# One transformer layer on eight cores: the mean of |W| for three weights is taken during attention and output projection, and the ternarizing of a weight strip is spread between token blocks

## The reference

```
x = x + attn(layernorm(x), Wq, Wk, Wv, Wo)      # 16 heads of 128, rope, causal softmax
x = x + ffn(layernorm(x), w_gate, w_up, w_down)  # d_ffn = 8192

def _weight_quant(w):                  # three values: -scale, 0, +scale
    scale = clip(mean(|w|), 1e-5)
    return clip(round(w / scale), -1, 1) * scale
def _act_quant(x):                     # 8-bit integers per token
    scale = 127 / clip(max(|x|, last axis), 1e-5)
    return clip(round(x * scale), -128, 127) / scale
ffn: gate = bl(x, w_gate); up = bl(x, w_up); out = bl(silu(gate) * up, w_down)
     where bl(x, w) = einsum(act_quant(x), weight_quant(w))
```

## Time and profile before

| | us |
|---|---|
| median of the runs before (2 runs, 11487.83 to 11526.1) | 11506.97 |
| the profiled execution | 11501.9 |
| its span, on the slowest core (core 3; the 8 cores: 11405.9 to 11500.3) | 11500.3 |
| attention, from 2421 us of the span | 2671 |
| output projection, from 5092 us | 585 |
| the means, from 5677 us | 697 |
| gate and up: first strip ternarized, from 6374 us | 179 |
| gate and up, from the first matmul at 6553 us | 2797 |
| down, from 9350 us | 2150 |

### The profile page before, as it was taken

One profiled execution on the slowest core, in us unless ns is written; L12 is line 12 of the kernel. 1 busy time (PEld: TensorE's weight loads), 2 busy tenths in 40 slices (PEclk: granted clock), 3 DMA queues, 4 the chain that ended last, 5 costly groups with the idle time before them and its releaser, 6 DMA issues.

```text
span 11500.3 us, 91991 instructions; the slowest of 8 cores (11405.9 to 11500.3 us)
## 1 busy us (share of the span) xinstructions
PE 5967.9 (52%) x23698; PEld 2265.1 (20%) x23698; DVE 4138.7 (36%) x5258; ACT 1951.3 (17%) x3620; POOL 1254.3 (11%) x587
## 2 busy tenths in 40 slices
PE   0025664965665566555200165756657556363737
PEld 0012221421111111112100022322323222131313
DVE  3513332132222222216675344444444441405050
ACT  4541110013333333331000000000000010101010
POOL 0002121000000000000000323233232300000000
PEclk9999898977777777777655587878878777575857
DMA  2251423310000000023496524233233313332333
GB/s 103 93 129 37 75 54 64 75 44 22 22 13 22 22 22 13 22 46 102 145 338 241 157 97 120 91 114 109 95 121 97 101 62 122 97 123 95 132 95 115
DMA packets 618721, 1048.40 MB, mean 91 GB/s; under 512 B 337394, under 2 KB 419314, under 8 KB 568818
## 3 DMA queue, kind: packets, MB, share of 16 engines
q1 hardware_dynamic: 441444, 656.54, 19.2%
q10 hardware_dynamic: 168192, 352.40, 8.9%
q0 software_dynamic: 8592, 33.59, 1.8%
HBM read 807.51 MB, written 218.10 MB: 89 GB/s over the span
## 4 chain that ended last, share of the span: by engine, by line
PE 36%; DVE 25%; DMA 11%; ACT 9%; issue 8%; POOL 6%; SPq 2%; ACTq 2%; DVEq 1%; another core or an unknown queue 1%; POOLq 0%
PE pb L68 27%; ACT p_E L68 3%; PE p2S L68 3%; DVE p_hqt L68 3%; PE p4b L68 3%; SPq L68 2%; ACT p_dump L68 2%; DVE p_pm L68 2%; DVE p4a_tmp L68 2%; DVE p_invr L68 2%; DVE p_wf L68 2%; DMA p_wf<-wgT 2%; ACTq L68 2%; DMA p4a_w<-wdT 2%; DMA p_wf<-wuT 1%
## 5 line engine op out<-in xcount | busy, mean ns | idle before, releaser
L68 PE MATMUL pb<-p_wgt,p_xiT 128*128 128x512 bf16 x4096 | 961.2, 389 | 1167.8 <-DVE p_ht L68 987.4
L68 PE MATMUL pb<-p_wds,p_hTg 128*128 128x512 bf16 x4096 | 999.5, 413 | 263.5 <-DMA p_wds<-wdtd 263.5
L68 ACT ACTIVATE p_E<-pb,p_negB 128x512 bf16<-128x512 f32 x1280 | 879.7, 687 | 788.6 <-PE pb L68 628.8
L68 PE MATMUL p2S<-p_E,g_ones_colb 128*1 128x512 bf16 x1280 | 539.1, 421 | 483.4 <-DVE p_E L68 254.8
L68 DVE TENSOR_TENSOR p_E<-p_E,p_masks 128x512 bf16<-128x512 bf16 x512 | 218.1, 426 | 1470.3 <-ACT p_E L68 1470.1
L68 PEld LDWEIGHTS pb<-p_wgt,p_xiT 128*128 128x128 bf16 x4096 | 408.3, 100 | 1681.2 <-issue 1221.9
L68 DVE TENSOR_SCALAR p_pm<-p_wf,p4a_invtau 128x2048 f32<-128x2048 f32 x192 | 407.7, 2123 | 718.5 <-DMA p_wf<-wdT 261.8
L68 PE MATMUL pb<-k_pp_xT,k_pp_W 128*128 128x512 bf16 x2048 | 476.9, 388 | 289.0 <-ACT k_pp_qb L68 185.2
L68 ACT ACTIVATE p_sg<-pb,p_cg 128x512 f32<-128x512 f32 x256 | 175.9, 687 | 2524.0 <-DVE p_cu L68 1559.9
L68 PEld LDWEIGHTS pb<-p_wds,p_hTg 128*128 128x128 bf16 x4096 | 426.0, 104 | 835.9 <-issue 571.6
L68 PE MATMUL pb<-p_qT,p_kT 128*128 128x512 bf16 x1280 | 560.1, 448 | 0.0
(11 more groups left out here) (158 smaller groups left out, 6652.3 us busy)
## 6 DMA issues: line engine op xcount, KB each, us to landing
p_wds<-wdtd ACTq DMA_DIRECT2D x128, 1024.0 KB, 5.2
p4a_w<-wgT SPq DMA_DIRECT2D x16, 4096.0 KB, 15.7
p4a_w<-wuT SPq DMA_DIRECT2D x16, 4096.0 KB, 15.2
p4a_w<-wdT SPq DMA_DIRECT2D x64, 1024.0 KB, 5.9
p_wf<-wdT SPq DMA_DIRECT2D x64, 1024.0 KB, 6.6
p_wf<-wgT SPq DMA_DIRECT2D x64, 1024.0 KB, 6.0
p_wf<-wuT SPq DMA_DIRECT2D x64, 1024.0 KB, 5.3
hfpd<-p_ht ACTq DMA_DIRECT2D x256, 256.0 KB, 2.0
```

What stands on the lines that cost most here:

```text
L68: real = getattr(eng, meth)(*a, **k)
```

## The change

Two things are changed.

The first: stage 4 is gone. Its sums are taken in 192 chunks of 128 x 2048, each by a load on SP (`wa_t`, two buffers), one ACT instruction with the function Abs that also gives the sum over the columns (`wa_tmp`), and one small ACT instruction that adds it (`wa_acc`). Five chunks are recorded at the end of each head in stage 2 and seven at the end of each token block in stage 3, 80 and 112 in all. The few instructions that turn the sums into thresholds come at the end of stage 3.

The second: in stage 5 the 12 items of strip fw+1 are no longer recorded ahead of the token blocks of strip fw, but one behind each of its first 12 blocks.

```diff
+    wa_state = {"i": 0, "rel": [(sS, 0), (sS, 0)], "first": True}
+    def wa_chunk(mi, wd, r0, c0, W):
...
+        slw = i % 2
+        sem = [dm["wa0"], dm["wa1"]][slw]
+        wait(Y, wa_state["rel"][slw])
+        sem.inc(Y.dma_start(wa_tile[slw][:, :W], wd.ap()[r0:r0 + 128, c0:c0 + W]), 16)
+        toks = [(sem, sem.v)]
...
+        wait(Sc, *toks)
+        sop("activation", wa_dump[:, :W], wa_tile[slw][:, :W], AF.Abs,
+            accum_out=wa_tmp[:])
+        wa_state["rel"][slw] = (sS, sS.v)
+        sop("activation", wa_acc[mi][:], wa_tmp[:], AF.Identity,
+            bias=wa_acc[mi][:], scale=1.0)
...
             hrel[sl] = (sT, sT.v)
+            wa_feed(5)
         barrier_all()
...
             xirel[sl] = (xisem[sl], xisem[sl].v)
+            wa_feed(7)
+        wa_feed(len(wa_items))
+        wa_epilogue()
         barrier_all()
...
-            if fw + 1 < DF // 512:
-                emit_tern(fw + 1)
+            pend = tern_items(fw + 1) if fw + 1 < DF // 512 else []
             terntok = terntoks[fw]
...
                     hstrel[eb] = (hsm, hsm.v)
+                    if pend:
+                        pend.pop(0)()
+            while pend:
+                pend.pop(0)()
+            if fw + 1 < DF // 512:
+                terntoks[fw + 1] = (sG, sG.v)
```

More of the change, by code:

```diff
@@ L529, in build_program @@
         return nc, st, RECS
+    wstats = {}
+    for mi in range(3):
+        wstats[mi] = (sb(f"p4a_swn{mi}", [128, 1], F32),
+                      sb(f"p4a_tau{mi}", [128, 1], F32),
+                      sb(f"p4a_invtau{mi}", [128, 1], F32))
+    p4as = ExitStack()
+    sba = lambda name, shape, dt: p4as.enter_context(nc.sbuf_tensor(name, shape, dt))
+    wa_tile = [sba(f"wa_t{i}", [128, 2048], F32) for i in range(2)]
+    wa_dump = sba("wa_dump", [128, 2048], F32)
+    wa_acc = [sba(f"wa_acc{i}", [128, 1], F32) for i in range(3)]
@@ new lines, in build_program @@
+    wa_tmp = sba("wa_tmp", [128, 1], F32)
+    wa_tot = sba("wa_tot", [1, 1], F32)
+    for mi in range(3):
+        gop("memset", wa_acc[mi][:], 0.0)
+    wa_state = {"i": 0, "rel": [(sS, 0), (sS, 0)], "first": True}
+    def wa_chunk(mi, wd, r0, c0, W):
+        i = wa_state["i"]
+        wa_state["i"] = i + 1
+        slw = i % 2
[3 more added lines that the diff above has]
+        toks = [(sem, sem.v)]
+        if wa_state["first"]:
+            toks.append((sG, sG.v))
+            wa_state["first"] = False
+        wait(Sc, *toks)
[4 more added lines that the diff above has]
+            bias=wa_acc[mi][:], scale=1.0)
@@ new lines, in build_program, with wa_feed, wa_epilogue @@
+    wa_items = []
+    for mi, (wdt, Rr, Cc) in enumerate([(d_wgT, D, DF), (d_wuT, D, DF),
+                                        (d_wdT, DF, D)]):
+        for ti in range(Rr // 128):
+            for c in range(Cc // 2048):
+                wa_items.append((lambda mi=mi, wdt=wdt, ti=ti, c=c:
+                                 wa_chunk(mi, wdt, ti * 128, c * 2048, 2048)))
+    def wa_feed(n):
+        for _ in range(n):
+            if wa_items:
+                wa_items.pop(0)()
+    def wa_epilogue():
+        for mi, (Rr, Cc) in enumerate([(D, DF), (D, DF), (DF, D)]):
+            b_swn, b_tau, b_invtau = wstats[mi]
+            wait(T, prel[5], (sS, sS.v))
+            top("matmul", pb[5][0:1, 0:1], wa_acc[mi][:], g_ones_col[:],
+                start=True, stop=True)
+            wait(Sc, (sT, sT.v))
+            sop("activation", wa_tot[:], pb[5][0:1, 0:1], AF.Identity)
+            wait(V, (sS, sS.v))
+            vop("tensor_scalar", wa_tot[:], wa_tot[:], 1.0 / (Rr * Cc), 1e-5,
+                ALU.mult, ALU.max)
+            wait(T, (sV, sV.v), (sS, sS.v))
+            top("matmul", pb[5][:, 0:1], g_ones_row[:], wa_tot[:],
+                start=True, stop=True)
+            wait(Sc, (sT, sT.v))
+            sop("activation", b_swn[:], pb[5][:, 0:1], AF.Identity,
+                bias=0.0, scale=-1.0)
+            wait(Sc, (sS, sS.v))
+            sop("activation", b_tau[:], pb[5][:, 0:1], AF.Identity,
+                bias=0.0, scale=0.5)
+            prel[5] = (sS, sS.v)
+            wait(V, (sS, sS.v))
+            vop("reciprocal", b_invtau[:], b_tau[:])
@@ L847, in build_program @@
             xirel[sl] = (xisem[sl], xisem[sl].v)
+            wa_feed(7)
+        wa_feed(len(wa_items))
+        wa_epilogue()
         barrier_all()
+    p4as.close()
     if upto == 4:
         return nc, st, RECS
[L853 to L902, removed]
```

31 lines of the change are left out of this document (20 added, 11 removed), and 3 rows, old and new, of the table dm.

## The result

| | us | of before |
|---|---|---|
| before, median of 10 runs (11440.77 to 11591.69) | 11496.58 | |
| after, median of 11 runs (11151.64 to 11246.67) | 11199.85 | 0.9733 [0.970, 0.9765] |

A forecast was written before the change was run, and what follows sets the result against it. No engine is busy throughout; barrier-cut stages are bounded by waits. Change one +163 us (attention +263, projection +588, means -688) and change two -437 took 11501.9 to 11228, rounded 11225; range for 8 in 10: 11000 to 11440.

The forecast's parts named there:

- The turn in attention: After PE's end of a head (E), next loads wait behind five chunks: 16.2 us late, 14 heads, 227 us; attention +263.
- the last head and the lump behind it: End of attention: exponents queue behind the fifth chunk, 18.7 us; the lump adds 17 ahead of the barrier.
- 3.6 us for each further megabyte in the queue: Load time on SP's queue, from 5.9 us for 1 MB and 15.7 for 4 MB.
- The projection: From ACT's last store (X), next block's loads wait behind seven chunks: 69 us a block for 31.6; +588 in all.
- The chunk: One chunk on ACT takes 2.5 us: a 1.91 us pass plus 0.6; its buffer is free after 2.0.
- allowance of 0.6: Per chunk on ACT: 0.6 us for reading the sum out, the small addition and waits, estimated by tiny products.
- Another function table: Rival: Abs needs another table than the exponent, two table loads of 1.283 us per lump, +82 us, 11307; chance 0.07.
- Change two: Gate and up: blocks 12.8 us with w_down items, 10.6 with other items, 3.6 without; strip 150.5, stage -437.
- The rival in which DVE slips past POOL: Gate and up: p_cg and p_cu start ahead of POOL in most blocks; strip 123 us, total 10810; chance 0.10.
- PE at its low level: Rival in gate and up: PE stays at 1.2 GHz after rests, deciding below granted clock 0.65; total 12280; chance 0.06.

The follow-up runs named there:

- e3: After with the loads of the next head and next token block issued on SP ahead of the lump's chunk loads; 10838.03 us, ratio 0.9426.
- e4: After with p_cg and p_cu taken once for all sixteen token blocks at the start of gate and up; 10825.3 us, ratio 0.9434.
- e5: e4 with block maxima written to columns of their own and reduced once at the stage's end, so no g_hamax in the blocks; 10702.75 us, ratio 0.9299.
- e1: After with its second part undone: chunks kept, a strip's items again ahead of its blocks; 11633.85 us, ratio 1.0102.
- e2: Before with only the second part: items spread between the blocks, means stage kept; 11085.04 us, ratio 0.9636.
- e7: After without the lumps: chunks summed by DVE inside attention's query windows, three buffers loaded ahead, none in the projection; 10364.26 us, ratio 0.9006.
- e6: e5 with ACT's four stores of an item, and the wait for POOL, recorded one block later behind the next silu; 10558.14 us, ratio 0.9178.
- e8: e6 with the means of e7; 9754.68 us, ratio 0.8461.

## Why the prediction was right

**The sum.** The mechanisms came as forecast in each stage that was changed. That the total is only 25 us off the median is in part luck: attention and projection came 12 and 18 us below their terms, gate and up 21 above, and these cancel.

**The turn in attention.** Forecast 16.2 us a head, measured 15.5: the loads of k, 14 of them from the third on, are issued 180.4 us apart in after ((5001.13 - 2655.47)/13) and 164.9 in before. The steps, in the turn shown: SP reaches the loads at E + 11.7 (12.4 forecast), DVE starts at E + 22.0 (23.8). The rest, the last head and the lump behind it, is 250.6 - 14 x 15.5 = 34 (35.7). e3 adds what the prediction did not say: as soon as SP's order is put right, the same lump delays the head through ACT's queue. The prediction's 3.6 us for each further megabyte in the queue doesn't follow from the two rows that it names, (15.7 - 5.9)/3 = 3.3; in the lump of the block below the passes that wait for their loads start 3.4 to 3.7 us apart, so the size did no harm.

**The projection.** Forecast 69.0 us a block, measured 68.3, from the stores of `xintd`, 16 of them:

```profile
L68 ACTq DMA_DIRECT2D xintd<-p_xi x16: 344/344/345, 5449.3 to 6474.3; - x16
```

(6474.3 - 5449.3)/15 = 68.3. The steps hold too: in the block behind X = 5791.97, `p_ct` is issued at X + 17.7 (18.4 forecast), the matmuls start at X + 24.8 (26.7), DVE's last addition ends at X + 42.8 (43.9) and the next X is at 68.2 (69.0). That SP's order is the cause is shown by e3, whose only difference here is that order, with 254 us.

**The chunk.** 2.5 us forecast; 1.91 + 0.19 + 0.29 with gaps are 2.48. The allowance of 0.6 was right in sum, though it was taken from small products: before has the instruction itself, an `ACTIVATION_READ_ACCUMULATOR` of 0.19 us behind each `p_dump<-p_x`. Another function table: the count of table loads stays 14, so that rival falls. The Trainium skill (ScalarE: Activation LUTs, Table sets: the hidden batching unit) agrees with the trace in that abs needs no switch. Its price for a switch was not tried.

**Change two.** Forecast 12.8 and 10.6 us for the item blocks and 3.6 for the rest, measured 12.96, 10.6 and 3.65 in the mean of 15 strips; a strip 151.9 by the working above, 151.4 from silu to silu, against 150.5. The rival in which DVE slips past POOL held for 4 blocks in 180. That POOL's subtraction holds DVE's small product, and not the count of DVE's instructions, is shown by e4 and e5: the instruction that is held changes with the one that stands beside POOL, and when no product with two inputs in SBUF is left the strip is down by 29 us. That what is held is a port is an explanation, no run shows it by itself; nor did a run separate the two inputs from the operation, since the small instructions that are held are all products of two tensors (TENSOR_TENSOR). The Trainium skill (SBUF — State Buffer, SBUF: two separate sides), which the prediction weighed, names that port pair and its lock. The trace agrees with it: a product of 128 elements waits for the rest of POOL's 4.51 us, up to 4.30, and `p_ht` with its input from PSUM is spared.

**PE at its low level.** It did start low after some of its short rests. Three first halves of item blocks in the timeline of after:

```profile
7340.14 5.28 PE L68 MATMUL pb<-p_wgt,p_xiT 128*128 128x512 bf16 x16 [2.18 <-DVE p_ht L68]
...
7353.04 5.30 PE L68 MATMUL pb<-p_wgt,p_xiT 128*128 128x512 bf16 x16 [4.17 <-DVE p_ht L68]
...
7363.64 3.61 PE L68 MATMUL pb<-p_wgt,p_xiT 128*128 128x512 bf16 x16 [1.85 <-DVE p_ht L68]
```

After rests of 2.18 and 4.17 us sixteen matmuls take 5.3 us, after 1.85 they take 3.6, the full rate. The mean of the stage is 0.93, far from the 0.65 at which it would decide, and a block that starts low still has time to spare beside DVE's 10.6.

**What was not foreseen.** The 75 us in down. They are in the profile, and most of them not in the medians. The down stage on the slowest core and its granted clock, one profile each: e1 2189 us at 0.68, before 2149 and e2 2155 at 0.69, e7 2117 at 0.70, after, e3, e4, e6 and e8 2071 to 2076 and e5 2082 at 0.72. The kernels with the first part of the change stand at both ends of that list (e1 and e4), and this stage is word for word the same in all. So it isn't the change. The cores of one execution differ as much. Two cores of before in down, core 0 and core 3, and ten microseconds of core 3 in it:

```profile
9350.00:11400.00 2050.00, 1049.83 (x5105) 505.33 (x5104) 590.67 (x706) 243.09 (x1080) 79.39 (x63) 0.72 0.34 114
9350.00:11400.00 2050.00, 1060.66 (x4864) 496.92 (x4864) 600.50 (x720) 240.25 (x1081) 71.76 (x57) 0.69 0.33 109
9810.00:9820.00 10.00, 10.00 (x39) 4.13 (x38) 0.00 (x0) 0.00 (x0) 0.00 (x0) 0.81 0.29 105
```

Cores 0, 1, 4 and 5 of before take 2075 to 2077 us for down (the cores of after 2076 to 2089) and never show 0.81 there. Cores 2, 3, 6 and 7 have a clock of 0.81 for 380 to 595 us of it, in stretches of matmuls, and take 2138 to 2174. In after no core has such a stretch. Core 3, with 464 us of them, loses 464 x 0.19 = 87 us at most, so they account for the 75; what brings them to two cores of a die and not to their neighbours stays open.

The two steps that failed are of the expectations. For e3, I left out that SP's wait for the head's end would now hold the chunk loads that used to be prefetched, and that ACT's lump, so delayed, would then hold the head: 88 us for the 200 expected. For e4, the 126 us a strip were not the sum of their terms, since the w_down blocks stay as long as they were.

## What to carry to other kernels

An engine with idle time is not free room: ask what is queued behind the added work on it, and behind its loads on the queue that issues them. Here lumps at a loop's turn cost more than their own passes: 15.5 us a head for five passes of 2.48 us, 36.6 us a block for seven. The same sums in single pieces inside the heads, on DVE and with their loads ahead, cost nothing. Beside a long POOL instruction keep every DVE product of two SBUF operands out of the chain, however small: take it once ahead, or write to columns and reduce later.

## What the runs showed of the hardware

The granted clock of a stage that no edit touched ranged from 0.68 to 0.72 over the profiles of these kernels, and from 0.68 to 0.72 over the cores of one execution of before. It moved the stage by up to 118 us, half of the 2% that counts as a difference. Compare stages, and the cores within them, before you compare spans.

A DVE instruction with a single large SBUF input is not always free of POOL either. The first compare of an item, in before and in after (min/median/max ns):

```profile
L68 DVE TENSOR_SCALAR p_pm<-p_wf,p4a_invtau x192: 1285/2406/3414, 6462.9 to 9139.3; 128x2048 f32<-128x2048 f32 x192
L68 DVE TENSOR_SCALAR p_pm<-p_wf,p4a_invtau x192: 1285/1286/2839, 6597.8 to 8942.2; 128x2048 f32<-128x2048 f32 x192
```

In before, where items follow each other closely, its median is 2406 ns, for 1286 in after, where POOL is done by then. In e8, with DVE early again, it is 2214. One such row of e8 beside POOL's:

```profile
6466.76 4.52 POOL L68 TENSOR_TENSOR p_wgt<-p_wf,p_pm 128x2048 bf16<-128x2048 f32 x1 [4.53 <-DVE p_wf L68]
...
6468.58 3.78 DVE L68 TENSOR_SCALAR p_pm<-p_wf,p4a_invtau 128x2048 f32<-128x2048 f32 x1 [0.45 <-DMA p_wf<-wgT]
```

The compare ends 1.08 us behind POOL, a little less than its own 1.29. So do the others: each first compare that starts while POOL is at work, 129 of 192 in before and 131 in e8, ends 1.08 to 1.20 us behind it, and each of the rest takes 1.29. The reduction `p_amx`, which also has one input in SBUF, is not held. In e8 the held compare costs nothing, since PE is the bound; in before it lay among waits for loads, and what it cost there wasn't tried.
